# Who makes the normalised rows and who adds the residual in the last stage of a language-model tower

## The reference

```
# 3: attention, heads of 4 channels, on _layernorm(h)
x = _layernorm(h)                       # "x2"
q, k, v = split(x @ W_qkv.T + b_qkv)    # 16 heads x 4
k, v = norm over the 4 channels (ddof=1) * w + b
kv  = einsum('bhnd,bhne->bhde', k, v) / 256
out = einsum('bhnd,bhde->bhne', q, kv)
h  += gelu((out + x) @ W_proj.T + b_proj, approximate=False) + x
# 4: half of the tokens through an MLP, on _layernorm(h)
x = _layernorm(h)                       # "x3"
w = x @ wr + br ; the 127 best tokens of each row are chosen
h += x + (chosen ? w * (gelu(x @ w1 + b1) @ w2 + b2) : 0)
```

## Time and profile before

| | |
|---|---|
| the three runs, median | 5116.01 us |
| profiled execution | 5124.35 us |
| its span | 5122.5 us |
| busy: PE matmul, PE weight load | 3072.0 us (60%), 2328.3 us (45%) |
| busy: DVE, ACT, POOL | 2808.3 us (55%), 2358.2 us (46%), 2231.7 us (44%) |
| granted TensorE clock, mean | 0.73 of full speed |
| DMA | 145.13 MB, mean 28 GB/s |

### The profile page before, as it was taken

One profiled execution on the slowest core, in us unless ns is written; L12 is line 12 of the kernel. 1 busy time (PEld: TensorE's weight loads), 2 busy tenths in 40 slices (PEclk: granted clock), 3 DMA queues, 4 the chain that ended last, 5 costly groups with the idle time before them and its releaser, 6 DMA issues. The chain is left out here.

```text
span 5122.5 us, 63233 instructions
## 1 busy us (share of the span) xinstructions
PE 3072.0 (60%) x21149; PEld 2328.3 (45%) x21149; DVE 2808.3 (55%) x5784; ACT 2358.2 (46%) x4288; POOL 2231.7 (44%) x2218
## 2 busy tenths in 40 slices
PE   3646663665565665665665665665665665625775
PEld 2435552554454454454454544544544544523443
DVE  8857882454454454454454454454544544558885
ACT  3635665444344344344344444444444443405775
POOL 7866613334434334344344344344344344435520
PEclk8667675777777777777777777777777777766776
DMA  2111101111111111111111111111111111112101
GB/s 58 24 22 21 21 6 44 24 23 34 24 26 27 28 27 31 24 27 31 23 27 31 23 27 31 23 27 31 23 27 30 23 32 26 21 44 55 54 2 33
DMA packets 157528, 145.13 MB, mean 28 GB/s; under 512 B 71240, under 2 KB 133080, under 8 KB 156776
## 3 DMA queue, kind: packets, MB, share of 16 engines
q1 hardware_dynamic: 88656, 109.49, 6.4%
q0 software_dynamic: 68768, 34.45, 6.1%
HBM read 92.97 MB, written 50.82 MB: 28 GB/s over the span
## 5 line engine op out<-in xcount | busy, mean ns | idle before, releaser
L937 PE MATMUL es_pgot<-hash_space,es_pick 128*128 128x256 bf16 x13056 | 1836.0, 288 | 1424.2 <-issue 1403.9
L857 POOL DMA_INDIRECT es_got<-node_table,late x1632 | 1551.7, 951 | 2124.4 <-DVEq L1077 1646.9
L937 PEld LDWEIGHTS es_pgot<-hash_space,es_pick 128*128 128x128 bf16 x13056 | 1299.8, 101 | 1903.6 <-issue 1747.5
L1019 DVE TENSOR_TENSOR es_prod<-es_pgot,es_own 128x512 f32<-128x512 f32 x272 | 187.8, 690 | 1800.7 <-PE es_pgot L937 1620.5
L871 ACT ACTIVATE es_pick<-es_away,consts 128x512 bf16<-128x512 f32 x1088 | 680.0, 711 | 7.0 <-DMA es_away<-sorted_keys 6.7
L293 POOL DMA_INDIRECT fr_ring<-in_emb,fr_rows x384 | 459.6, 1197 | 203.5 <-issue 112.5
L875 ACT ACTIVATE es_pick<-es_pick,consts 128x4096 bf16<-128x4096 bf16 x136 | 503.6, 3703 | 0.9
L894 ACT ACTIVATE ex_hid<-ex_phid,weights 128x256 f32<-128x256 f32 x128 | 53.8, 471 | 707.6 <-PE ex_phid L944 707.3
L1039 DVE TENSOR_TENSOR es_hot<-es_iota,late 128x1024 bf16<-128x1024 f32 x272 | 331.6, 1219 | 35.4 <-DVE es_st L1079 25.7
L1040 DVE TENSOR_TENSOR es_hot<-es_iota,late 128x1024 bf16<-128x1024 f32 x272 | 330.1, 1214 | 0.0
L910 ACT ACTIVATE ex_y<-ex_py 128x512 f32<-128x512 f32 x64 | 38.2, 597 | 574.6 <-remote 553.3
(11 more groups left out here) (351 smaller groups left out, 4334.8 us busy)
## 6 DMA issues: line engine op xcount, KB each, us to landing
es_away<-sorted_keys SPq DMA_DIRECT2D x68, 512.0 KB
es_got<-node_table,late POOLq DMA_INDIRECT x1632
edge_states<-es_st SPq DMA_DIRECT2D x68, 384.0 KB
expert_outputs<-ex_y SPq DMA_DIRECT2D x64, 256.0 KB
bk_y<-expert_outputs SPq DMA_DIRECT2D x8, 2048.0 KB
fr_ring<-in_emb,fr_rows POOLq DMA_INDIRECT x384
out_dram<-h SPq DMA_DIRECT2D x4, 1024.0 KB, 5.1
late<-in_edges SPq DMA_DIRECT2D x1, 2048.0 KB, 9.0
```

Of the source, the lines that this page charges most:

```text
L857: pool.indirect_dma_start(out=got[:, r, k, :], out_offset=None, in_=table_dram, in_offset=bass.IndirectOffsetOnAxis(ap=src[:, n, k:k + 1]. ...
L937: mm = pe.matmul(p_got[:, q, c * 256:c * 256 + 256], pick[:, r, q // 2, k, at * P:at * P + P], parts[:, part, k], start=(k == 0 and part = ...
```

## The change

Four things, all in `back`:

1. GpSimd multiplies xc by the reciprocal roots for x2 and x3, where VectorE did. VectorE keeps the reciprocals, which now release two new semaphores, `rstd2` and `rstd3`. The second norm's reciprocal stands at the head of VectorE's step, ahead of part 0 of the gates; the first norm's (`root_back`) stands at the end of the fourth step, behind the new `rt`.
2. GpSimd's step begins with x3 of slot n-3 and ends with x2 of slot n+1; the gathers and additions are between.
3. VectorE makes `rt` as attention's output (read from PSUM) plus xt; ScalarE's copy of it goes, and so do TensorE's two products of xt with the projection weights (four passes in the profile).
4. ScalarE does attention's gelu behind the MLP's gelu and ahead of x3t.

In GpSimd's program:

```
+            def second_rows(s):
+                pool.wait_ge(s_rstd2, s // GS + 1)
+                if s >= 2:
+                    pool.wait_ge(s_hx2, s - 1)
+                    pool.wait_ge(s_xt_p, s - 1)
+                nc.gpsimd.tensor_tensor(x2[:, s % 2], by_half(xc[:, slot(s)]), by_half(spread(rstd2[:, slot(s)], D)), ALU.mult).then_inc(s_x2, 1)
             for n in range(-10, 0):
                 gathers(n, range(ST))
+            second_rows(0)
             for n in range(STEPS):
                 new, normed, mlp = n, n - 1, n - 3
+                if is_slot(mlp):
+                    pool.wait_ge(s_rstd3, mlp + 1)
+                    if mlp >= 2:
+                        pool.wait_ge(s_hx3, mlp - 1)
+                        pool.wait_ge(s_x3_p, mlp - 1)
+                    nc.gpsimd.tensor_tensor(x3[:, mlp % 2], by_half(xc[:, slot(mlp)]), by_half(spread(rstd3[:, slot(mlp)], D)), ALU.mult).then_inc(s_x3, 1)
                 gathers(n, range(2))
...
+                if is_slot(new + 1):
+                    second_rows(new + 1)
```

In ScalarE's program:

```
                     if new >= 2:
-                        act.wait_ge(s_prj_p, new - 1)
+                        act.wait_ge(s_rt, new - 1)
                     a.activation(xt[:, new % 2], p_xt, ACT.Copy).then_inc(s_xt, 1)
...
+                if is_slot(joined):
+                    act.wait_ge(s_prj_p, joined + 1)
...
+                    a.activation(gj[:, joined % 2]..., p_prj, ACT.Gelu).then_inc(s_gj, 1)
...
-                if is_slot(normed):
-                    act.wait_ge(s_o_p, normed + 1)
...
-                    a.activation(rt[:, normed % 2], p_o, ACT.Copy).then_inc(s_rt, 1)
```

In VectorE's program:

```
+            def root_back(g):
+                dve.wait_ge(s_std2, g + 1)
+                v.reciprocal(rstd2[:, tiles(g)], rstd2[:, tiles(g)]).then_inc(s_rstd2, 1)
+            root_back(0)
             for n in range(STEPS):
-                if is_slot(new):
...
-                    v.tensor_tensor(x2[:, new % 2], by_half(xc[:, slot(new)]), by_half(spread(rstd2[:, slot(new)], D)), ALU.mult).then_inc(s_x2, 1)
+                if is_slot(mlp):
+                    dve.wait_ge(s_std3, mlp + 1)
+                    v.reciprocal(rstd3[:, slot(mlp)], rstd3[:, slot(mlp)]).then_inc(s_rstd3, 1)
                 gates_at(q, 0, g)
...
-                if is_slot(mlp):
-                    dve.wait_ge(s_std3, mlp + 1)
-                    do(v.reciprocal(rstd3[:, slot(mlp)], rstd3[:, slot(mlp)]))
...
-                    v.tensor_tensor(x3[:, mlp % 2], ..., ALU.mult).then_inc(s_x3, 1)
...
+                if is_slot(normed):
+                    dve.wait_ge(s_o_p, normed + 1)
+                    if normed >= 2:
+                        dve.wait_ge(s_prj_p, normed - 1)
+                    v.tensor_tensor(rt[:, normed % 2], p_o, xt[:, normed % 2], ALU.add).then_inc(s_rt, 1)
+                if q == 3 and g + 1 < GN:
+                    root_back(g + 1)
                 gates_at(q, 2, g)
```

In TensorE's program:

```
-                    for half in range(2):
-                        pe.matmul(p_prj[:, half * P:half * P + P], xt[:, normed % 2, half * P:half * P + P], W("proj_w"), start=False, stop=False)
```

More of the change, by code:

```diff
@@ L1308, in back @@
             sem(n) for n in ("xtp", "kvp", "qp", "kvmp", "op", "prjp", "x3p", "hidp", "ytp", "yp", "rwp"))
-        s_hx2, s_kv, s_hx3, s_sd = (sem(n) for n in ("hx2", "kv", "hx3", "sd"))
+        s_hx2, s_kv, s_hx3, s_sd, s_rstd2, s_rstd3 = (sem(n) for n in ("hx2", "kv", "hx3", "sd", "rstd2", "rstd3"))
         s_var_g, s_std_g, s_less, s_exp, s_read, s_xc2, s_sq2, s_sum2, s_std2, s_used = (
@@ L1429, in _ @@
                     gate_squares(g + 1)
+                if is_slot(joined):
+                    act.wait_ge(s_prj_p, joined + 1)
+                    if joined >= 2:
+                        act.wait_ge(s_xc3, joined - 1)
+                    a.activation(gj[:, joined % 2].rearrange("p two b d -> p (two b d)"), p_prj, ACT.Gelu).then_inc(s_gj, 1)
                 if is_slot(mlp):
@@ L1437, in _ @@
                     a.activation(sq_kv[:], groups(new), ACT.Square).then_inc(s_sq, 1)
[L1438 to L1442, removed]
                 if is_slot(last):
@@ L1447, in _ @@
                     a.activation(yt[:], p_yt, ACT.Identity, bias=W("m_b2")).then_inc(s_yt, 1)
-                if is_slot(normed):
-                    act.wait_ge(s_o_p, normed + 1)
-                    if normed >= 2:
-                        act.wait_ge(s_prj_p, normed - 1)
-                    a.activation(rt[:, normed % 2], p_o, ACT.Copy).then_inc(s_rt, 1)
                 if q == 3 and g + 2 < GN:
```

## The result

| | before | changed |
|---|---|---|
| median of the runs on the same chip, us | 5113.95 (4 runs, 5108.48 to 5119.61) | 5151.15 (4 runs, 5149.93 to 5159.95) |
| ratio | | 1.007, 95% interval 1.0051 to 1.0089: slower, by 0.7% |
| profiled execution, span, us | 5124.35, 5122.5 | 5151.96, 5150.2 |

The forecast was 5151, in the range 5119 to 5170. The median rose by 37.2 us.

A forecast was written before the change was run, and what follows sets the result against it. The prediction took a loop of waits between engines, none of them full, as the bound. Terms 35.0 - 4 - 2 + 3 + 3 + 0 gave +35 us, 5151 against the median 5116.01; range 5119 to 5170.

The forecast's parts named there:

- The reciprocal at the head: VectorE's step: part 0 falls between ScalarE's root and the heads' reciprocal, +5.83 us per four steps, +35.0 in all.
- Gelu and rt: ScalarE before its query eviction: early gelu and no rt copy gain little, TensorE's chain being untouched; -4, bounds 0 and -29.
- q = 3: The step in four with the exp: its table load no longer stands behind rt on ScalarE, a gain of 0.4 us.
- the sign that the prediction named: In the changed profile, ScalarE's query eviction would be released by TensorE in every step, if the forecast was right.
- The shared port: GpSimd's added operations hold VectorE's through SBUF, each by about 0.5 us: +3, bounds 0 and 12.
- The five steps without part 0: Steps 27 to 31, without the gates' part 0: only the gain of early gelu and rt is left, -2, bounds 0 and -6.
- Ramp-up: First steps: GpSimd is late, x2 of slot 1 stands behind four slow gathers; +3, bounds 0 and 6.
- Behind step 32: Ramp-down: three steps with slower x3 and one more hand-over, +1, earlier gelu, -1; 0, give or take 2.
- TensorE's fewer passes: Four passes less on TensorE, behind the query eviction's start and in front of nothing late: 0.
- Quick TensorE: Rival: TensorE at its quick pace, heads' reciprocal to query eviction falls by the full bound; +6, time 5122, chance 0.13.
- VectorE's queue: Rival: VectorE reaches its step's head after ScalarE's root, so its lesser work counts; 29 us less, 5087, chance 0.12.
- GpSimd's queue: Rival: blocked operations and gathers make GpSimd's step the longest, x2 late; 24 to 31 us more, about 5180, chance 0.08.

The follow-up runs named there:

- The wait alone: Kernel before with only the second norm's reciprocal and its wait moved ahead of the gates' part 0: 5178.55 us against 5146.75, ratio 1.0069.
- Gelu alone: Kernel before with only the gelu and its table load ahead of x3t: 3408.85 us against 3423.81, ratio 0.9952; on another chip 5107.06, ratio 0.9975.
- gelu with rt on VectorE: Kernel before with the gelu early, rt made on VectorE, TensorE's two xt products gone, norms' rows kept on VectorE: 5135.8 us against 5146.75, ratio 0.9985.
- the kernel with the wait behind part 0: Changed kernel with only the second norm's reciprocal moved behind the gates' part 0: 5152.8 us against the kernel before's 5146.75, ratio 1.0011.
- the rows alone: Kernel before with both norms' rows on GpSimd and the second norm's reciprocal behind the gates' part 0: 5156.99 us against 5146.75, ratio 1.0023.
- the repeat of the changed kernel: Changed kernel, unedited, timed again on one more chip: 5153.37 us against the kernel before's 5121.02, ratio 1.0064.

## Why the prediction was right

*The reciprocal at the head, +35.0.* Right in mechanism and size. S to R was forecast at 1.34, 1.82, 2.66, 2.67 (ending at q = 3, 0, 1, 2) and came at 1.05, 1.81, 2.60, 2.60; +32.8 in 24 steps. The wait alone gives +33.0, and taking it behind part 0 takes 29.7 away. The cover that it lost is ScalarE's way to S: part 0 used to be done in it.

*Gelu and rt, -4.* The net size was near: K to Q got 1.07 us shorter for four steps, 6.4 in 24. The value of the edit and the reason were not right. Gelu alone takes 13.6 to 13.8 us off the 24 steps (over three times the term), gelu with rt on VectorE 9.0. The step that failed is "TensorE's own chain from keys-times-values to queries is untouched, so Q moves only where ScalarE was the later". In the kernel before, that chain itself waits for ScalarE: the transposes of the MLP output (L1747) stand ahead of the queries and need ScalarE's L1447, which stood behind the gelu and its table load. The waits of their weight loads for it from 4700 to 5040 us, before and then with the gelu alone:

```profile
PEld bk_pxt L1747 <- ACT bk_yt L1447: 16.6, 23, 1.5
```

```profile
PEld bk_pxt L1747 <- ACT bk_yt L1447: 4.3, 11, 0.6
```

With most of that wait gone, the granted clock of the steady stretch also rose, from 0.76 to 0.82; the prediction had this as a bound and a rival, and left it at nothing. How much each of the two gave, no run separates.

That the changed kernel got 6.4 us and not 13.7 has another reason than the one that the prediction gave, so here its number is near by luck. It said that TensorE would wait longer in front of keys times values and so stay at the slow pace, and the trace after has the longer wait (77.6 us against 46.0). But the wait alone lengthens it to 74.7 us, and the clock from 4690 to 5000 us stays at 0.76 and R to Q at 37.14. And the kernel with the wait behind part 0 has it back at 46.0, with the gelu early, and yet the clock is 0.75 and K to Q 25.09, no shorter than the 24.72 before. It differs from the kernel with gelu and rt (clock 0.79, K to Q 22.89) by the rows on GpSimd and by the reciprocal's place behind part 0, so the gain is lost with those two, without any longer wait; the rows alone, without the gelu, have 0.75 and 25.29. A part to be seen is TensorE's wait for the head mask, 13.0 and 13.4 us in the two kernels with the rows moved and the wait behind, against 4.9 before. What keeps TensorE slow there stays open.

The parts don't add up either: gelu with rt (-9.0) and rows on GpSimd (+5.8) would give -3.2 in the 24 steps, but together, with the wait behind part 0, they gave +3.6. Of these 6.8 us, K to Q holds +9.8 (25.09 where the two effects added give 23.46) and S to R -3.1 (2.50 where they give 3.01). Why is open.

The Trainium skill (ScalarE: Activation LUTs, What ACT_TABLE_LOAD costs) has a drain of 1.38 us beside the load. The trace after doesn't show it: the gelu starts 0.01 us after its load ends, on ScalarE.

```profile
4885.39 1.28 ACT L1451 ACT_TABLE_LOAD   x1
4886.68 0.38 ACT L1451 ACTIVATE bk_gj<-bk_pq 128x256 f32<-128x256 f32 x1
```

*q = 3.* The prediction counted a gain of 0.4 there, with the exp's table load no longer behind rt. K to Q at q = 3 is unchanged (7.02, 7.04), while the gelu alone takes it to 6.67. The row is L1398 above: it waits 1.66 us for data that VectorE makes behind the new rt, and the query eviction stands behind it, so that at q = 3 this eviction isn't released by TensorE, against the sign that the prediction named.

*The shared port, +3, bounds 0 to 12.* Right in place. The products are held for 1.16 us in four steps, +7.0 in 24, 0.72 of the 1.16 at q = 3; that is 4 more than forecast. But what the delay is worth on the loop is less: without it 1.9 and 2.9 us came back, about the 3. The prediction doesn't tell the two apart.

*The five steps without part 0, -2.* They came at 62.81 from step 27 to 32 against 63.04, -0.2, and at 64.82 in the repeat of the changed kernel, so even the sign isn't firm. The gain of the gelu is real (59.54 with rt and 59.54 alone). The port takes 1.3 of it, since the three products are 2.34 us in place of 2.07; the rest is lost in K to Q, as in the 24 steps.

*Ramp-up, +3*: R of step 1 to step 3 took 23.15 against 20.46, +2.7. The number came, its mechanism hardly. TensorE did wait for x2 from GpSimd, 5.7 us in front of slot 1's transposes, but that wait lies almost wholly ahead of R of step 1, and slot 0's keys times values still began 0.3 us after their products; for slot 2 it was 0.7 us. But the reciprocal alone makes the stretch 21.49, the rows on GpSimd alone 21.46, and gelu with rt on VectorE, without any rows on GpSimd, 22.14, where the gelu alone has 20.67. So at most 1.0 of it is the rows, and rt on VectorE with TensorE's fewer passes, which the prediction put at nothing, costs about 1.5 there. *Behind step 32*: -0.5, forecast 0. *TensorE's fewer passes, 0*: not tried by themselves. Together with rt on VectorE they made the 24 steps 4.7 to 4.9 us longer than the gelu alone (313.70 against 309.02 and 308.83), so that pair is a loss, of which the passes' share is open.

The sum in `back` is 33.3 + 2.7 - 0.2 - 0.5 = 35.3, which is the 35.2 above but for rounding, where 35 was forecast. That the figure is so near owes much to errors that cancel: the port is 4 too small and the last five steps 2 too good, the gelu 2 too weak and the first term 2 too large. That the median came within 0.2 us of 5151 is luck besides, since the four runs of the kernel before lie 11 us apart. The profiled execution was forecast at 5159.4 and took 5151.96, as the stages ahead of `back` ended 7.55 us earlier. Of the +53 at the range's upper end, 6 are the gelu's two terms at nothing, which the text there doesn't name.

*The rivals.* Quick TensorE: not here, since R to Q hardly moved (37.23 to 37.32), though half of its bound appeared with the gelu alone. VectorE's queue: it idles 1.6 to 2.8 us at its head in the steps above, far from the point where that rival decides. GpSimd's queue: it waits 150.7 us for the reciprocal, once in each of the 24 steps, so it doesn't end last there.

## What to carry to other kernels

In an in-order queue a small instruction with a wait sets the place of everything behind it: put independent work ahead of it, as long as it fits into the wait. Before you move work to an idle engine, look at what its operands must pass through; here two products moved to GpSimd, 0.42 us each on VectorE and 0.61 us or more there, bought nothing and held others. Moving a table load and its gelu out of the late part of ScalarE's step was the one good part. Taking the bad wait away didn't bring its gain out; only running it by itself did.

## What the runs showed of the hardware

- Where GpSimd's vector operations meet VectorE's products of two SBUF inputs, the one that starts second waits for the end of the first. In the changed kernel's trace 19 of the keys' and values' products start inside a GpSimd vector operation, and each ends 0.55 to 0.56 us after that operation; in the rows of the experiment with both norms' rows on GpSimd it is 5032.26 against 5031.72. On the other side seven of GpSimd's operations start inside VectorE's [128, 2048] addition, and each ends 0.47 us after it. One is x3's product, 0.61 us in the rows of that experiment, beside the addition that ends at 4929.72:

```profile
4927.62 2.57 POOL L1374 TENSOR_TENSOR bk_x<-xc,bk_rstd 128x256 f32<-128x256 f32 x1 [5.41 <-DVE bk_rstd L1642]
```

  The delay is the rest of the other's operation, so it can be anything from 0.1 to 2 us. The 1.16 us product at q = 3 doesn't fit: it starts 0.5 us before GpSimd's addition and inside a gather, and is back at 0.69 when the addition is moved away. What held it is open.
- The same kernel took 3423.81 us on one chip and 5113.95 to 5146.75 on three others, while the 24 steps of the two kernels run on both kinds agree within 1.2 us (354.05 and 352.91, 308.83 and 309.02). The difference lies in the earlier stage where edges are gathered. Its row in the gelu alone, on a slow chip and then on the quick one (what, count, busy us, mean ns, idle before, released by):

```profile
L857 POOL DMA_INDIRECT es_got<-node_table,late x1632 | 1548.0, 949 | 2126.4 <-DVEq L1077 1649.1
```

```profile
L857 POOL DMA_INDIRECT es_got<-node_table,late x1632 | 1582.8, 970 | 497.4 <-issue 497.4
```

  In the one, GpSimd stands idle 2126 us, 1649 of them released by VectorE's sequencer; in the other 497 us. Why, no run here shows.
